# Gated mLSTM and mixture of experts on one core: load order, q's masked copies on ScalarE, gates turned earlier

## The reference

```python
q = layernorm(x); k = v = ctx
ig = [q,k,v] @ Wi + bi ; fg = [q,k,v] @ Wf + bf          # 16 heads each
F  = cumsum(log_sigmoid(fg)); log_D = F[s] - F[t] + ig[t]   (t <= s)
D  = exp(log_D - max);  C = (q k^T / 4) * D
h  = C / max(|sum C|, exp(-max)) @ v, normed per head, * ln_scale
x  = x + tanh(g_xattn) * h
```

## Time and profile before

| | us |
|---|---|
| median of 3 runs (250.07, 253.47, 253.7) | 253.47 |
| the profiled execution | 250.66 |
| its span, first to last instruction | 248.8 |
| PE busy | 205.4 |
| DVE busy | 142.4 |
| POOL busy | 106.1 |
| ACT busy | 93.0 |

### The profile page before, as it was taken

How to read it: one execution, slowest core, us unless ns; L and a number is a source line. 1 busy time by engine, 2 the same in 40 slices (tenths; PEclk the granted TensorE clock), 3 DMA queues, 4 the chain that set the end, 5 groups by cost and what they waited for, 6 DMA issues and landing times.

```text
span 248.8 us, 4136 instructions
## 1 busy us (share of the span) xinstructions
PE 205.4 (83%) x1294; PEld 147.4 (59%) x1295; DVE 142.4 (57%) x316; ACT 93.0 (37%) x178; POOL 106.1 (43%) x102
## 2 busy tenths in 40 slices
PE   8393968999958768327799999999999999999950
PEld 3172833444423544213588888888888888888840
DVE  4389297599996957887868777322333223322220
ACT  0550325665553383400366575322323223232310
POOL 7056008888562400005106564465544654455222
PEclk9979899999997858755899999999999999999997
DMA  5959999900020112201102233222432233332321
GB/s 143 253 192 322 378 370 377 362 35 1 3 77 8 44 43 86 86 0 54 30 3 42 45 55 67 49 43 42 66 63 42 42 46 59 59 46 42 31 34 21
DMA packets 20031, 23.40 MB, mean 94 GB/s; under 512 B 3888, under 2 KB 15152, under 8 KB 20016
## 3 DMA queue, kind: packets, MB, share of 16 engines
q1 hardware_dynamic: 12640, 15.89, 19.0%
q0 software_dynamic: 4464, 6.16, 15.5%
q10 hardware_dynamic: 2912, 1.15, 1.7%
HBM read 17.95 MB, written 5.24 MB: 93 GB/s over the span
## 4 chain that ended last, share of the span: by engine, by line
PE 64%; DVE 19%; DMA 5%; ACT 4%; issue 3%; ACTq 2%; POOL 1%; DVEq 0%; POOLq 0%
PE bank L1251 26%; PE bank L1268 15%; PE bank L1082 4%; PE bank L1260 4%; DMA wg_sb<-in_L_xattn_Wf_dram 3%; PE bank L1006 3%; PE bank L1119 2%; DVE arena L720 2%; PE bank L1233 2%; PE bank L1143 2%; DMA out_dram<-hraw,sidx 2%; PE bank L1098 1%; DVE xn_sb L806 1%; PE bank L1052 1%; ACTq L446 1%
## 5 line engine op out<-in xcount | busy, mean ns | idle before, releaser
L436 POOL DMA_INDIRECT out_dram<-hraw,sidx x23 | 37.6, 1637 | 63.3 <-DVE hraw L966 60.3
L1251 PE MATMUL bank<-arena_r,xn_sb_r 128*128 x184 | 57.2, 392 | 0.0
L960 DVE TENSOR_TENSOR x_sb<-x_sb,bank 128x512 f32<-128x512 f32 x23 | 15.8, 688 | 57.3 <-ACT x_sb L594 57.3
L1268 PE MATMUL bank<-w_sb,xn_sb 128*128 x184 | 43.6, 380 | 0.8 <-ACT xn_sb L598 0.8
L1251 PEld LDWEIGHTS bank<-arena_r,xn_sb_r 128*128 128x128 f32 x184 | 34.8, 189 | 7.1
L1251 PE MATMUL bank<-w_sb_r,xn_sb_r 128*128 x92 | 38.4, 417 | 0.4 <-DVE w_sb_r L858 0.4
L1268 PEld LDWEIGHTS bank<-w_sb,xn_sb 128*128 128x128 f32 x184 | 33.2, 190 | 4.6 <-issue 1.0
L594 ACT ACTIVATE x_sb<-bank 128x512 f32<-128x512 f32 x23 | 13.7, 597 | 49.4 <-PE bank L1251 49.4
L390 POOL TENSOR_SCALAR_AFFINE_SELECT arena<-arena 128x1024 f32<-128x1024 f32 x16 | 18.1, 1134 | 25.9 <-ACT arena L494 25.8
L419 POOL DMA_INDIRECT cvT<-xnorm_scratch,gidx x12 | 12.0, 1004 | 29.3 <-DVE gidx L918 26.0
L598 ACT ACTIVATE xn_sb<-bank 128x512 f32<-128x512 f32 x23 | 13.8, 598 | 25.8 <-PE bank L1260 25.8
(11 more groups left out here) (183 smaller groups left out, 270.6 us busy)
## 6 DMA issues: line engine op xcount, KB each, us to landing
w_sb<-in_L_ffn_w_dram SPq DMA_DIRECT2D x24, 512.0 KB, 9.1
x_sb<-in_x_dram SPq DMA_DIRECT2D x2, 512.0 KB, 7.3
arena<-in_ctx_dram ACTq DMA_DIRECT2D x2, 512.0 KB, 10.7
xnorm_scratch<-xn_sb SPq DMA_DIRECT2D x8, 128.0 KB, 1.8
out_dram<-x_sb SPq DMA_DIRECT2D x8, 128.0 KB, 1.8
out_dram<-hraw,sidx POOLq DMA_INDIRECT x23, 3.8
cvT<-xnorm_scratch,gidx POOLq DMA_INDIRECT x12, 2.9
hc<-xnorm_scratch,gidx POOLq DMA_INDIRECT x11, 2.8
```

Of the source, the lines that this page charges most:

```text
L436: nc.gpsimd.indirect_dma_start(out=out[:, :], out_offset=bass.IndirectOffsetOnAxis(ap=sidx[:, i:i + 1], axis=0), in_=y_sb[i % 2], in_offse ...
L960: nc.vector.tensor_tensor(h_sb[p], sg_sb[p], ps_scores[p][:, 1, :], ALU.mult).then_inc(s_hm, 1)
L1251: last = nc.tensor.matmul(ps_scores[p][:, n, :], a, w, start=(k == 0 and j == 0), stop=(k == KC - 1 and j == 2))
L1268: last = nc.tensor.matmul(ps_tr[:, 0:H], hT_sb[p][:, k * P:(k + 1) * P], w2_sb[:, bass.ds(e * W2 + k * H, H)], start=(k == 0), stop=(k == ...
```

## The change

It has these parts:
- SyncE issues x (two halves) and then the context (two halves), the biases, the scale and the router weights, and goes on to the expert weights without a wait.
- ScalarE's queue holds the two gains and then the gate weights, under a semaphore of their own (`s_wg`). VectorE waits for it before the fold, and for `s_par` (now four transfers) only before it adds the biases.
- VectorE takes both halves' statistics first, and ScalarE makes both guesses first.
- `mask_q` leaves GpSimd. ScalarE makes the copies, one head at a time, as Copy activations of 128x256 with the head's mask column as the scale: 32 instructions in place of 8. Each sequence's four are placed in ScalarE's list, those of b = 0 and 1 in the gate stage, the others in rounds b = 0 to 5 of the loop, two sequences ahead.
- TensorE turns each half's gates directly after the step behind their matmul: `turn_gates(0)` ahead of pairs 6 and 7, `turn_gates(1)` ahead of `center_v(2)`.

```diff
-            for i in range(2):
-                sp.dma_start(x_sb[...], x_tok[...]).then_inc(s_x[i], 16)
+            for dst, src, done in ((x_sb, x_tok, s_x), (ctx_sb, c_tok, s_c)):
+                for i in range(2):
+                    sp.dma_start(dst[:, HB * i:HB * (i + 1), :], src[:, HB * i:HB * (i + 1), :]).then_inc(done[i], 16)
...
-            sp.wait_ge(s_par, 16 * NPAR)
             for e in range(E):
                 experts(e)
...
# GpSimd
-            def mask_q(b):
-                pool.wait_ge(s_qks, Q_STORED[b // 2])
-                nc.gpsimd.tensor_tensor(qm[:, b], qkT[:, b, 0:KC, :]..., pmask..., ALU.mult).then_inc(s_qm, 1)
...
-            EARLY = 4
-            pool.wait_ge(s_pm, 1)
-            for b in range(EARLY):
-                mask_q(b)
             for b in range(B):
                 mask_decay(2 * b)
                 mask_decay(2 * b + 1)
-                if b + EARLY < B:
-                    mask_q(b + EARLY)
...
# ScalarE
-            for i in range(2):
-                act.dma_start(ctx_sb[...], c_tok[...]).then_inc(s_c[i], 16)
-            act.dma_start(wg_sb[:, :, 0:NH], ...).then_inc(s_par, 16)
-            act.dma_start(wg_sb[:, :, NH:G2], ...).then_inc(s_par, 16)
+            act.dma_start(wg_sb[:, :, 0:NH], ...).then_inc(s_wg, 16)
+            act.dma_start(wg_sb[:, :, NH:G2], ...).then_inc(s_wg, 16)
...
+            def mask_q(b, heads):
+                act.wait_ge(s_qks, Q_STORED[b // 2])
+                for h in heads:
+                    nc.scalar.activation(qm[:, b, :, h, :], qkT[:, b, 0:KC, :], ACT.Copy,
+                                         scale=pmask[:, h:h + 1]).then_inc(s_qm, 1)
...
             guess_ln(0)
+            guess_ln(1)
             store_pair(0, 1, 0)
...
             store_pair(3, 0, 1)
-            guess_ln(1)
...
             store_pair(7, 0, 3)
+            act.wait_ge(s_pm, 1)
+            mask_q(0, (0,))
             store_gT(1)
+            mask_q(0, (1, 2))
             softplus()
+            mask_q(0, (3,))
+            mask_q(1, (0, 1))
             upper_a(0)
             upper_a(1)
             decay(0)
+            mask_q(1, (2, 3))
             decay(1)
... (in the loop over b, after store_cv(b - 1) and guess_heads(g))
+                if b + 2 < B:
+                    mask_q(b + 2, (0, 1))
                 if 2 * b + 3 < 2 * B:
                     decay(2 * b + 3)
... (after store_cvT(b) and square_heads(g))
+                if b + 2 < B:
+                    mask_q(b + 2, (2, 3))
                 if 2 * b + 4 < 2 * B:
                     decay(2 * b + 4)
...
# VectorE
             ln_stats(0)
+            ln_stats(1)
             ln_apply(0)
-            dve.wait_ge(s_par, 16 * NPAR)
+            dve.wait_ge(s_wg, 32)
             nc.vector.tensor_tensor(wg_sb[...]...).then_inc(s_par2, 1)
-            ln_stats(1)
             ln_apply(1)
...
             store_v(1)
+            dve.wait_ge(s_par, 16 * NPAR)
             dve.wait_ge(s_gt, 2)
...
# TensorE
-                    pe.wait_ge(s_qm, b + 1)
+                    pe.wait_ge(s_qm, 4 * b + 4)
...
             center_v(0)
+            turn_gates(0)
             turn_pair(6, xn_sb, 2)
             turn_pair(7, xn_sb, 3)
-            turn_gates(0)
             center_v(1)
             gates_of(1)
+            turn_gates(1)
             center_v(2)
-            turn_gates(1)
             center_v(3)
```

More of the change, by code:

```diff
@@ L211, in bass_gated_mlstm_moe_kernel @@
         s_par = sem("params_loaded")
+        s_wg = sem("gate_weights_loaded")
         s_w = [sem("first_experts_loaded"), sem("last_experts_loaded")]
@@ L298, in bass_gated_mlstm_moe_kernel @@
         HB = B // 2
-        NPAR = 6
+        NPAR = 4
         NG = B // 2
@@ L314, in _ @@
         def _(sp):
-            for i in range(2):
-                sp.dma_start(x_sb[:, HB * i:HB * (i + 1), :], x_tok[:, HB * i:HB * (i + 1), :]).then_inc(s_x[i], 16)
+            for dst, src, done in ((x_sb, x_tok, s_x), (ctx_sb, c_tok, s_c)):
+                for i in range(2):
+                    sp.dma_start(dst[:, HB * i:HB * (i + 1), :], src[:, HB * i:HB * (i + 1), :]).then_inc(done[i], 16)
             sp.dma_start(gb_sb[:, 0:NH], bi.rearrange("(a h) -> a h", a=1).to_broadcast([P, NH])).then_inc(s_par, 16)
@@ L378, in _ @@
             pool.dma_start(out[T:T + P, :], zrow[:, :]).then_inc(s_dump, 16)
-            def mask_q(b):
-                pool.wait_ge(s_qks, Q_STORED[b // 2])
-                nc.gpsimd.tensor_tensor(qm[:, b], qkT[:, b, 0:KC, :].unsqueeze(2).to_broadcast([P, KC, 4, S]),
-                                        pmask[:, :].unsqueeze(1).unsqueeze(3).to_broadcast([P, KC, 4, S]),
-                                        ALU.mult).then_inc(s_qm, 1)
             def mask_decay(n):
@@ L444, in _ @@
             act.dma_start(gx[:, 1:2], g_ffn.rearrange("(a b) -> a b", a=1).to_broadcast([P, 1])).then_inc(s_g, 16)
-            for i in range(2):
-                act.dma_start(ctx_sb[:, HB * i:HB * (i + 1), :], c_tok[:, HB * i:HB * (i + 1), :]).then_inc(s_c[i], 16)
-            act.dma_start(wg_sb[:, :, 0:NH], wi.rearrange("(c p) h -> p c h", p=P)).then_inc(s_par, 16)
-            act.dma_start(wg_sb[:, :, NH:G2], wf.rearrange("(c p) h -> p c h", p=P)).then_inc(s_par, 16)
+            act.dma_start(wg_sb[:, :, 0:NH], wi.rearrange("(c p) h -> p c h", p=P)).then_inc(s_wg, 16)
+            act.dma_start(wg_sb[:, :, NH:G2], wf.rearrange("(c p) h -> p c h", p=P)).then_inc(s_wg, 16)
             act.wait_ge(s_g, 32)
```

## The result

| us | before | after |
|---|---|---|
| median (4 runs each, same chip) | 252.16 (250.07 to 253.7) | 241.85 (241.49 to 243.05) |
| profiled execution | 250.66 | 241.57 |
| its span | 248.8 | 239.8 |
| mean granted TensorE clock | 0.918 | 0.930 |

The ratio is 0.9652 [0.9609, 0.9695]: faster, as forecast, but by more: the median lies 4.4 us under the 246.2 predicted and 0.15 under the low end of the range. Part of that is the starting point: with a fourth run the median before is 252.16 and not the 253.47 that the forecast started from, and 0.9652 of 253.47 would be 244.7. The span is 9.0 us shorter. Executions of one kernel differ along with the clock they are granted: of 13 more of the kernel before, those at 0.912 to 0.918 took 250.56 to 251.87 us, those at 0.893 to 0.906 252.74 to 254.35.

What follows compares the result with a forecast made beforehand. The prediction took the gate stage to bound the first 30 us, with VectorE's root refinement slowed during GpSimd's masks. 250.66 - 6.4 + 0.5 = 244.8, plus half the 2.8 step between runs, gave 246.2 us; range 242 to 250.3.

Steps and rivals of the forecast that it cites:

- step 1: Gate stage, transfers: x lands no later than now, context's first half at 10.5 us, its second half some 13.5.
- step 2: Gate stage, ScalarE: table load still starts at 8.72, root guesses end at 12.4, first store at 12.4 instead of 12.90.
- this rival: Gate stage, ScalarE starts earlier: table load by 6 us, 1.5 us more saved, 244.7 us; chance 0.2.
- step 3: Gate stage, VectorE: second root refinement takes 0.6 us, second half of xn ready at 16.2 instead of 24.4.
- step 4: Gate stage, TensorE: `gates_of(0)` ends at 17.8 instead of 18.3, gates biased at 23.3 instead of 29.76.
- The bounds, -4.9 to -8: Gate stage gain: -4.9 us if the low clock falls on pairs 6, 7 and later work, -8 if ScalarE starts earlier.
- The masks' price: ScalarE's 32 masked copies: 0.50 us each, 0.41 back to back, 13.1 in all; 0 to 0.3 exposed in the gate stage.
- The loop, +0.5: Attention loop: every second decay 0.8 us late, free in the first two rounds; net +0.5, range -1.1 to +2.5.
- ScalarE bounds the loop: Attention loop rival: late decays delay the next difference, four rounds lose 0.8 each, +3.2 for +0.5, 248.9 us; chance 0.2.
- Expert weights earlier, 0: Expert weights issued some 8 us earlier gain 0, as ScalarE first reads them after the attention loop.
- The step between runs, +1.4: Whole kernel: median of runs 2.8 us above the profiled execution; half of it taken, from 244.8 to 246.2 us.

Runs made afterwards that it cites:

- masks-back kernel: The changed kernel with only the masked copies of q given back to GpSimd, everything else as after: 246.98 us, ratio 0.9796 to the kernel before.
- masks-only kernel: The kernel before with only the masked copies of q moved to ScalarE, all 32 at the places of after: 245.57 us, ratio 0.9783.

## Why the prediction was right, and where its sizes were off

The mechanism was right, and four terms of the sum carry the difference. On the profiled execution's clock it said -6.4 and +0.5; it was -8.2, +0.8 and -1.5: 250.66 - 8.9 = 241.8, against 241.57 run.

- *Landings (step 1).* Context's first half was there at 10.80 (10.5 taken); x needed 6.8 us, no more than before. Right.
- *ScalarE's start (step 2).* "I leave the start as it is" was the step that failed in the gate stage. The first load began at 4.39, not at 8.72, and ran while ScalarE waited for the gains, so that the first root guess came at 9.84 instead of 11.53. The reason given against this rival held: the gains needed 7.0 us to land (1.28 + 7.0 = 8.3, when Tanh starts). That agrees with the rule of the Trainium skill cited there (DMA: Bandwidth & Descriptors, "Queues, rings and completion order"). But the wait held back only Tanh and the second load, not the first. First store 11.60, not 12.4: 0.8 of the 1.8 missed in this stage. I had given this rival 0.2 and 1.5 us.
- *VectorE (step 3).* The cause was right: with the masks back on GpSimd the collisions return. That xn's second half came at 16.0 (16.2 predicted) is partly luck: the first half was refined at 10.80, not 12.0, and VectorE then idled 1.08 us for Wf. The weights "have until 14 us": they landed at 13.8. Being issued 3 us earlier, with only the gains ahead of them in their queue, moved them by 0.3: 11.4 us from issue to landing.
- *TensorE (step 4).* `gates_of(0)` ended at 16.7, not 17.8: 0.8 by the first store, and 0.3 by a shorter ping-pong behind it (4.06 from the store to `gates_of(0)`, before 4.36). Then the sum had `gates_of(1)`, a store and a turn behind two centrings; it measured 21.55 from 16.7, 4.9, where I had 5.5. The bounds, -4.9 to -8, missed it by 0.2: the range had no case with both the earlier start and the shorter path behind it.
- *The masks' price.* 0.50 long as predicted and 0.40 apart (0.41). In the gate stage they cost nothing visible: from the bias to the first `cvT` 13.73 us, before 13.75.
- *The loop, +0.5.* It was +0.8 (before the clock), near in size, but by another path, so the nearness is luck. I had priced a decay 0.8 late, at nothing in the first two rounds, where each round lost 0.2 from the first on; the chain shows TensorE waiting for the second mask pair itself, which was made directly ahead of the scores that read it. The move of that pair, with all 32 masks still on ScalarE, gave it back. The rival *ScalarE bounds the loop* had 3.2 us for it and was further off.
- *Expert weights earlier, 0.* It came out so, but the reason given looked only at who reads the expert weights, and not at what they hold up. Here the gate weights were issued before them and still landed in time: the fold ran at 13.84, `gates_of(0)` at 15.66. Whether their 11.4 us (8.7 before) come from the expert weights was not tried in this kernel. With the old queue the same edit cost 4.8 us (the two kernels with context on ScalarE). A throttle that I costed at nothing had protected a small transfer.
- *The clock at the end of the loop.* No term stood for it. 1.5 us came from the step b = 5 to 6, where the granted clock was 1.00 instead of 0.81. It follows no part of the change: the masks-back kernel has the short step (69.02 to 75.96, 6.94), and so has the masks-only kernel (6.98), while the kernel with context on ScalarE and the wait, whose masks are all on ScalarE, has the long one (8.50, at 0.80). With one profiled execution of each it may be chance, and the cause stays open.
- *The step between runs, +1.4.* The median after lies 0.3 above its profiled execution, before 1.5. Taking half of the 2.8 was 1.1 too much.

Together: 1.8 (gate stage) - 0.3 (loop) + 1.5 (clock) + 1.1 (step) = 4.1 of the 4.4 us missed.

## What to carry to other kernels

When small operations of VectorE show the length of a neighbouring GpSimd operation, move the GpSimd work before touching the order: that was over half of this gain. Once the masks were gone from GpSimd, taking back one of the two reorderings moved the gates by 0.2 and 0.6 us; with them on GpSimd, both together moved the gates by 1.15. Before you remove a wait that only holds back bulk transfers, ask which small transfer in another queue is still in flight. And make an operand well ahead of its reader: the loop's masks cost 2.3 us when half of them were made right before the scores that read them, and 0.4 with all of them half a round earlier.

## What the runs showed of the hardware, unexpected

- The 48 KB transfer of Wf took 8.7 to 17.1 us to land, by what ran beside and ahead of it: 8.7 and 8.9 behind context, with the expert weights held back (before, and the kernel with the added wait); 17.1 in the same place with the expert weights running; 11.4 with only the gains and Wi ahead of it and x, context and the expert weights in the other queue (after).
- The table load of ScalarE is done ahead of the wait for the operation's operand: 4.39 to 5.67 us, Tanh at 8.32.
- A masked copy of 128x256 by an ACTIVATE with a pointer scale takes 0.499 us and, back to back, 0.40 (four in 1.70), where GpSimd needed 1.86 for 128x1024: 1.70 against 1.86 for the same copies, and no VectorE operation of the gate stage grew beside them (logf, which has two inputs, took 0.29 us in both kernels).
